# Identity transposes up to both seams of `expert_choice`, its bias as one fp32r product, its output statistics on ScalarE, late weight groups between its tiles

## The reference, cut to what matters

```python
def _L0_ffn_ref(x, router_w, router_b, expert_w, expert_b):
    logits = xf @ router_w + router_b
    S = jax.nn.softmax(logits, axis=-1)
    G, idx = jax.lax.top_k(S.T, k)              # 16 experts, k = 64 of 1024 tokens
    tokens = xf[idx]
    out = jnp.einsum('ekh,hd->ekd', tokens, expert_w) + expert_b
    weighted = G[..., None] * out
    y = jnp.zeros((bs, h), dtype=x.dtype).at[idx.reshape(-1)].add(weighted.reshape(-1, h))
...
x = x + _layernorm(_L0_ffn_ref(_layernorm(x, axis=-1), ...), axis=-1)
```

## Time and profile before

| | |
|---|---|
| median of 3 runs | 509.27 us (508.12 to 510.45) |
| the profiled execution | 510.88 us |
| its span, first to last instruction | 509.1 us |
| mean granted TensorE clock | 0.834 |
| busy: PE, PE weight loads, VectorE, ScalarE, GpSimd | 388.3, 301.1, 301.4, 242.1, 112.3 us |
| time mixing | up to 81.8 us of the span |
| `expert_choice` | 82.3 to 139.1 us |
| `delta_attention` | from 139.6 us |

### The profile page before, as it was taken

The page is one execution under the profiler, slowest core; times in us unless marked ns, Lnnn a source line. Parts: engine busy times, 40 slices in busy tenths (PEclk is TensorE's granted clock), DMA queues, the critical chain, the costliest instruction groups (busy, mean ns, idle before and its releaser), DMA issues. The chain is left out here.

```text
span 509.1 us, 9989 instructions
## 1 busy us (share of the span) xinstructions
PE 388.3 (76%) x4106; PEld 301.1 (59%) x4106; DVE 301.4 (59%) x649; ACT 242.1 (48%) x427; POOL 112.3 (22%) x132
## 2 busy tenths in 40 slices
PE   2999775999379977543218799952999999999990
PEld 1544565756267766522117545642888888888880
DVE  5899997371832665699994467686394311311126
ACT  2889754103334677566314356655855422222330
POOL 5490001000000001500005500000034565334540
PEclk9999988555868999955558957995899999999996
DMA  7890000000000000000000000000004400000002
GB/s 224 254 303 1 0 1 0 1 1 0 0 0 3 1 3 3 1 1 1 0 0 3 3 5 4 3 2 0 1 2 166 165 1 2 1 1 0 2 1 82
DMA packets 12489, 15.82 MB, mean 31 GB/s; under 512 B 2046, under 2 KB 10644, under 8 KB 12444
## 3 DMA queue, kind: packets, MB, share of 16 engines
q1 hardware_dynamic: 12444, 15.18, 9.3%
HBM read 14.09 MB, written 1.08 MB: 30 GB/s over the span
## 5 line engine op out<-in xcount | busy, mean ns | idle before, releaser
L2191 POOL TENSOR_TENSOR hidden_r<-third,hidden_r 128x512 fp32r<-128x512 f32 x31 | 41.2, 1331 | 141.7 <-ACT hidden_r L2143 141.7
L2256 DVE TENSOR_TENSOR third<-third,ps 128x512 f32<-128x512 f32 x32 | 22.0, 686 | 84.8 <-PE ps L2074 79.5
L2090 PEld LDWEIGHTS ps<-down_r,hidden_r 128*128 128x128 f32 x384 | 49.1, 188 | 3.2 <-POOL hidden_r L2191 0.9
L2090 PE MATMUL ps<-down_r,hidden_r 128*128 128x256 f32 x384 | 50.2, 280 | 0.7 <-POOL hidden_r L2191 0.7
L2074 PE MATMUL ps<-xm_r,gate_r 128*128 128x512 f32 x192 | 50.1, 397 | 0.0
L2074 PE MATMUL ps<-xm_r,up_r 128*128 128x512 f32 x192 | 49.9, 396 | 0.0
L2143 ACT CAST hidden_r<-third 128x512 fp32r<-128x512 f32 x32 | 19.9, 623 | 59.2 <-PE ps L2090 59.2
L2074 PEld LDWEIGHTS ps<-xm_r,up_r 128*128 128x128 f32 x192 | 36.9, 192 | 7.9
L1475 PE MATMUL ps<-ident,area 128*128 128x128 f32 x32 | 8.4, 413 | 40.4 <-DVE area L1801 40.4
L2074 PEld LDWEIGHTS ps<-xm_r,gate_r 128*128 128x128 f32 x192 | 34.5, 191 | 5.8 <-issue 0.2
L1475 PEld LDWEIGHTS ps<-ident,area 128*128 128x128 f32 x32 | 5.5, 207 | 43.2 <-DVE area L1801 43.2
(11 more groups left out here) (324 smaller groups left out, 845.6 us busy)
## 6 DMA issues: line engine op xcount, KB each, us to landing
stored<-share_dram SPq DMA_DIRECT2D x8, 512.0 KB, 5.4
stored<-in_L_ffn_sw_dram SPq DMA_DIRECT2D x3, 1024.0 KB
stored<-in_L_ffn_w_dram SPq DMA_DIRECT2D x1, 2048.0 KB
x<-L_attn_hidden_state_dram SPq DMA_DIRECT2D x4, 256.0 KB, 3.7
out_dram<-x SPq DMA_DIRECT2D x4, 256.0 KB, 2.5
w_nat<-in_L_attn_Wk_dram SPq DMA_DIRECT2D x1, 256.0 KB, 2.9
w_nat<-in_L_attn_Wv_dram SPq DMA_DIRECT2D x1, 256.0 KB, 3.1
w_nat<-in_L_attn_Wr_dram SPq DMA_DIRECT2D x1, 256.0 KB, 3.3
```

The source lines that it names most:

```text
L2090: last = nc.tensor.matmul(ps[:, t // 2, t % 2 * D:(t % 2 + 1) * D], hidden_r[:, n % 2, hp, t * P:(t + 1) * P], down_r[:, wp, a, :], start= ...
L2191: nc.gpsimd.tensor_tensor(hidden_r[:, n % 2, LO, :], hidden[:, n % 4, :], hidden_r[:, n % 2, HI, :], ALU.subtract).then_inc(hidden_lo, 1)
L2256: V.tensor_tensor(hidden[:, n % 4, :], gated[:, n % 2, :], ps[:, 4 + 2 * (n % 2) + 1, :], ALU.mult) \
```

## The change

- **First seam.** Time mixing ends with 40 transposes of the identity and not 24; `expert_choice` begins on TensorE with 14.
- **Second seam.** The transposes at the end of `expert_choice` are 30 and not 36, and wait for the first normalized tile of the output (`tail_normed`); `delta_attention` begins with 8.
- **Bias.** GpSimd splits the fp32 bias into three parts that fp32r holds exactly, in rows 0, 32 and 64 of `bias_r`, and makes `bias_rows`, which has ones in these rows and zeros elsewhere. The bias of a tile is then one fp32r product. `experts(0)` waits for the ten GpSimd instructions. `to_quarters` and `minus_before` are now made behind these, in `expert_choice`.
- **Late groups.** One group stands ahead of each of tiles 2 to 6, none behind tile 7.
- **Statistics.** ScalarE passes over each pair of finished tiles with `Identity` and sums (`accum_out`) the means, between its copies of the late groups; when all eight are there it makes the negative means (`z_centre`), and then passes over the tiles with `Square` and sums the variances. VectorE no longer takes them.
- The semaphores of the logarithm and the reciprocal of time mixing become one.

```diff
-        STAY_WARM = 24
+        STAY_WARM = 40
...
-    STAY_WARM = 36
+    STAY_WARM = 14, 30
...
+        z_moments = sem("z_moments")
+        bias_made = core.pool_count[0] + 10
+        masks_made = bias_made + 1 + QUARTERS
...
+                for n in range(STAY_WARM[0]):
+                    nc.tensor.transpose(ps[:, 7, 0:P], core.ident[:], core.ident[:])
...
-                    nc.tensor.matmul(z[:, t], core.ones[0:1, :], core.b_ec[0:1, 0:D], start=False, stop=True) \
+                    nc.tensor.matmul(z[:, t], bias_rows[:], bias_r[:], start=False, stop=True) \
                         .then_inc(z_done, 1)
 
+                pe.wait_ge(sem("masks_order"), bias_made)
                 experts(0)
...
-                for t in range(1, NT):
+                experts(1)
+                for n, t in enumerate(range(2, NT)):
+                    core.turn_groups(pe, core.turned_late[n:n + 1], LATE_BANKS)
                     experts(t)
-                core.turn_groups(pe, core.turned_late, LATE_BANKS)
-
+
+                pe.wait_ge(sem("masks_order"), masks_made)
                 pe.wait_ge(ties_counted, 1)
...
-                for n in range(STAY_WARM):
+                pe.wait_ge(sem("tail_normed"), TB + 1)
+                for n in range(STAY_WARM[1]):
                     nc.tensor.transpose(ps[:, PROB_BANK, 0:P], core.ident[:], core.ident[:])
...
+                link(nc.gpsimd.tensor_copy(bias_r[:], bias))
+                subtract(rest[:], bias, bias_r[:])
+                link(nc.gpsimd.tensor_copy(bias_r[own[1]], rest[own[1]]))
+                link(nc.gpsimd.tensor_copy(bias_r[own[2]], rest[own[2]]))
+                subtract(bias_r[own[2]], rest[own[2]], bias_r[own[2]])
+                link(nc.gpsimd.memset(rest[:], 0.0))
+                for q in range(3):
+                    link(nc.gpsimd.memset(rest[PAD * q:PAD * q + 1, 0:P], 1.0))
+                link(nc.gpsimd.tensor_copy(bias_rows[:], rest[:, 0:P]))
...
-                core.keep_groups(act, core.turned_late, LATE_BANKS)
+                for n, t in enumerate(range(0, NT, 2)):
+                    act.wait_ge(z_done, t + 2)
+                    for tile in (t, t + 1):
+                        nc.scalar.activation(xf[:, tile], z[:, tile], ACT.Identity, scale=1.0 / D,
+                                             accum_out=norm.mv[:, tile, 0:1]).then_inc(z_moments, 1)
+                    core.keep_groups(act, core.turned_late[2 * n:2 * n + 2], LATE_BANKS)
+                act.wait_ge(z_moments, NT)
+                nc.scalar.activation(centre[:], norm.mv[:, :, 0], ACT.Copy, scale=-1.0 / D ** 0.5) \
+                    .then_inc(z_moments, 1)
+                act.wait_ge(z_moments, NT + 1)
+                for t in range(NT):
+                    nc.scalar.activation(xf[:, t], z[:, t], ACT.Square, scale=1.0 / D ** 0.5, bias=centre[:, t:t + 1],
+                                         accum_out=norm.mv[:, t, 1:2]).then_inc(z_moments, 1)
                 norm.on_act(act, core.ln_eps[:])
...
-                dve.wait_ge(z_done, NT)
-                for t in range(NT):
-                    last = norm.tile_stats(z, t)
-                link(last)
-                link(norm.gather_stats())
+                dve.wait_ge(z_moments, 2 * NT + 1)
                 dve.wait_ge(limit_and_g, 2)
...
+    STAY_WARM = 8
...
+                    for n in range(STAY_WARM):
+                        nc.tensor.transpose(ps[:, 0, 0:P], ident[:], ident[:])
```

More of the change, by code:

```diff
@@ L172, in masks @@
         g = self.nc.gpsimd
-        count = [0]
-        def link(ins):
-            count[0] += 1
-            ins.then_inc(order, 1)
-            pool.wait_ge(order, count[0])
+        link = chain(pool, order, self.pool_count)
         def where(dst, op, fill, base, pattern, step):
@@ L800, in expert_choice @@
         limit = sb("limit", [P, 1])
+        centre = sb("z_centre", [P, NT])
+        to_quarters = sb("to_quarters", [PAD, P])
+        rest = sb("bias_rest", [P, D])
+        bias_r = own.enter_context(nc.sbuf_tensor("bias_r", [P, D], F32R))
+        bias_rows = own.enter_context(nc.sbuf_tensor("bias_rows", [P, P], F32R))
+        minus_before = sb("minus_before", [P, P])
         own_least = sb("own_least", [P, QUARTERS])
@@ L2303, in sandwich @@
         core.norm_after = Norm(core, "ln_after")
-        core.dve_count = [0]
+        core.dve_count, core.pool_count = [0], [0]
         core.weights(ins)
```

30 lines of the change are left out of this document (16 added, 14 removed).

## The result

The changed kernel takes **487.36 us** (median of 4 runs, 484.04 to 490.06), the kernel before beside it on the same chip 508.69 (4 runs, 506.31 to 510.45): a ratio of 0.958 with a 95% interval of 0.950 to 0.966. The profiled execution of after took 489.34 us (span 487.6), that of before 510.88 (509.1): 21.5 us less, where 16.9 were forecast. In the medians of this document a run that lies over 1.5% above the fastest of its kernel is counted (one of `n_groups`, 495.62, and one of `n_stats`, 493.72), in the ratios it is not.

What follows compares the result with a forecast made beforehand. TensorE at half clock was taken to bound expert_choice; 15.9 us there plus 1.0 at the second seam made 16.9, giving 494.0 from the profile or 492.4 from the median, so 493.0 us, range 487.5 to 501.5.

Steps and rivals of the forecast that it cites:

- Second seam: From expert_choice into attention: first projections nearer full clock, between 0 and 3.2 us gained, 1.0 taken.
- the sum for `expert_choice`: Root of the variances at the stage's end done at 114.8 instead of 130.72, 15.9 us sooner.
- it is not the bound: VectorE's selection in expert_choice: scan ends at 107.3, `tied` near 109, so VectorE does not set the end.
- Half-clock stretch: Behind the router's logits TensorE runs 3.3 us at half clock, losing 1.6 us.
- Tiles: Expert tiles on TensorE: 1.1 us each at full clock, 2.2 at half; the last ends at 106.2.
- Sums on ScalarE: Statistics passes over the expert tiles: 0.67 us each, bounds 0.47 and 1.07; 8.6 us from last tile to root.
- (d): Rival: ScalarE's sums each end in a drain and read, making the kernel slower, 513.3 us at pitch 1.4; chance 0.04.
- (b): Rival: no half-clock stretch behind the logits and a warm second seam, 488.6 us; chance 0.11.
- Table load: ScalarE's load before the root: 1.28 us, no drain added, no cover assumed.
- (a): Rival: clock falls at the first seam anyway and rises after some 7 us of tiles, 499.5 us; chance 0.20.
- (c): Rival: half clock throughout expert_choice's tiles and groups, gain 3.3 us, 506.0 us; chance 0.09.
- (e): Rival: TensorE stops for ScalarE's copies or GpSimd, losing 16 us, within 0.5% of 509.3; chance 0.04.

Runs made afterwards that it cites:

- n_groups: Changed kernel with the five late groups behind the last tile again, copied by ScalarE between sums and squares: 489.92 us.
- n_stats: Changed kernel with the outputs' statistics back on VectorE, groups still between the tiles: profiled expert_choice stage 38.83 us.
- n_seam1: Changed kernel without the first seam's added transposes (24 at time mixing's end, none at the head of expert_choice): 493.1 us.
- v_attn: Changed kernel with 16 and 24 identity transposes filling TensorE's two pauses in the attention stage: 482.33 us.
- b_bias: Kernel before with only the bias as one fp32r product: 14.0 us off the stage, 15 off the kernel.
- n_bias: Changed kernel with the old one-row fp32 bias product, operands for the new one still made: 500.97 us.
- x_select: Changed kernel with two of eight selection rounds on VectorE left out, so the output differs: `limit` 1.95 us and the root 0.66 us sooner.
- after_again: The changed kernel run once more, unaltered, to see the spread: 487.79 us.
- n_seam2: Changed kernel with the old second seam: 36 transposes that wait for nothing, none at the attention stage's head: 489.24 us.
- v_tail: Changed kernel with 28 more transposes between the last tile and the products for `limit`, and 58 instead of 30 at the stage's end: 487.70 us.
- b_seam1: Kernel before with only the first seam's transposes (40 and 14): logits 4.47 us sooner, stage 5.23 us shorter.

## Where the prediction was right, and where it failed

The sign and the two large mechanisms stood: the seam's clock, and the bias that keeps the clock down. The size did not: 493.0 us were forecast and 487.36 measured, 0.14 us below the range. The step that failed is the sum for `expert_choice`: 15.9 us were to be gained there and 20.4 were. It had three faults. TensorE's last tile was put 3.0 us too late, the sums on ScalarE behind it were priced 2.1 us too high, and "it is not the bound", of VectorE, did not hold in this execution.

**First seam: right.** Logits 4.4 us sooner was forecast, and 4.47 measured. The 16 transposes took 2.05 us (1.9), the 32 products 3.71 (3.7), the half-clock stretch behind them 3.3. `n_seam1` gives all of it back.

**Half-clock stretch: priced too high.** "3.3 us at half lose 1.6" took the stretch to lie on the tiles. It lay on 90.0 to 93.3, where TensorE ran tile 0 ahead of need and then waited for the probabilities; from tile 1, at 92.86, on it cost some 0.4. That it was as short as forecast is in part luck: in four other executions it is 6.8 us and the last tile some 2 us later, which moves the root by 1.2 us (28.97 in `v_attn`, 27.75 in after). With the long one the stage gains 19.0 to 19.2 us and not 20.4, still over 3 more than forecast.

**Tiles: right in kind, a little high.** 1.1 us a tile and 1.57 with a group were forecast, 0.98 and 1.42 measured: 0.9 us over the seven tiles and five groups. The 0.24 us taken for an fp32 pass was an upper bound; the passes of a tile in after start 0.21 apart. From the logits to tile 1 it took 2.78 us (90.08 to 92.86), and not the 3.6 that were carried over. Of these 0.8 us TensorE itself was 0.6: in the kernel before the probabilities were ready at 97.68 and it came to them at 98.31, behind tile 0's old bias product; in after it was 92.32 and 92.38. With the stretch, the last tile ended 20.9 us into the stage and not 23.9: 3.0 us.

**Bias: right in kind, and the largest part.** `b_bias` alone brings 14.0 us of the stage; `n_bias` shows that it is the clock far more than the product. The forecast said as much, but gave no share.

**Sums on ScalarE: mis-sized.** I took 0.67 with 0.47 as the lower bound. Measured: sums 0.37 apart, squares 0.45 to 0.46 (the eight of them and the reads end at 107.23). The read of the accumulator that rival (d) feared is there, 0.19 to 0.24 us, but it overlaps the next activation. The bound came from an activation with two per-partition operands; those with one or none are faster here. Squares ended 4.9 us behind the last tile and not 7.0.

**"It is not the bound": wrong where the last tile is early.** VectorE's scan came nearly as worked out: it ended 24.4 us into the stage, and was forecast 25.0. But with the last tile 3.0 us and the squares 2.1 us earlier than I had them, ScalarE's chain ended ahead of VectorE's: the selection and the pick products behind `limit` end last, by some 0.6 us, and that only because the clock fell among these products at 107.0. They took 0.93 + 0.99 us, where `x_select` has 0.61 + 0.61. In the executions with the long stretch ScalarE's chain ends last, as forecast. From the end of the last tile to the root done it took 7.1 us, where 8.6 were forecast: 1.5 less, and not 2.1.

Together 3.0 + 1.5 = 4.5 us: 20.4 measured in the stage, 15.9 forecast. In the profiled executions 0.9 more came from the earlier start of the stage, which is spread, and 0.7 less from the second seam. The other 1.0 us of the 5.6 is in the medians: that of after lies 1.98 us below its profiled execution, where 493.0 allowed 1.0. On which side of the range's end the median fell is chance, too: after_again gives 487.79, just inside. But the range had been drawn too high. Its lower end had no case with both the cheap sums and the cheap stretch; rival (b) with the bare pass of 0.47 is 486.6.

**GpSimd: right.** The bias operands were ready at 88.15, and no row of TensorE waits for them. **Second seam: open.** The head of the attention stage gained 3.3 us, just beyond my upper bound of 3.2; over the stage 0.3 was left, against 1.0 taken; by runs 1.45 us lie between `n_seam2` and after_again, whose runs overlap. **Table load: right.** No drain shows: in `x_select` ScalarE's last read ends at 107.67, the load starts at 107.69 and the root at 108.98, 1.29 us later. The Trainium skill ("ScalarE: Activation LUTs", "What ACT_TABLE_LOAD costs") has about 1.38 us of drain with each such load; this trace has no room for it. In after the load ends at 108.53, ahead of the root at 109.15, so that it cost nothing there.

**Rivals.** (b), 488.6, is nearest to the measured time, though not by its reason: the half-clock stretch was there. (a) is what `n_seam1` shows when forced, at 493.1 and not 499.5: there too the tiles ended 3.4 us sooner and the rest took 2.1 us less than (a) had. (c) did not come; `n_bias`, at 500.97 and not 506.0, is nearest to it, with the clock at 0.50 for 20.3 us. (d) falls with pitches of 0.37 and 0.46. (e) falls with TensorE's 8.70 busy us of 8.70.

## What to carry to other kernels

When TensorE is slow over a whole stage, look for the cheap odd instruction in its steady loop as well as for the pause ahead of it: a pass that keeps the clock down costs far more than its own row says. An edit that shortens one of two chains to the same join can bring nothing until both are short, so price them as a pair, and redo the question of who ends last with the lower bounds as well as the chosen values. Filling a pause of TensorE paid where long work followed it (`v_attn`), and cost where a late start had already taken up the pause (`v_tail`). And where the clock falls at other places in the next execution, compare two profiles only when their stretches at half clock are alike.

## What the runs showed of the hardware that was not expected

- One-row fp32 products between full ones kept TensorE at 0.50 for 20.3 us in which it waited for no other engine (`n_bias`), where the same tiles without them run at 1.00 from 93.4 on (after). The bias products of the eight tiles are all that differs. Their weights, and those of what follows them, are not loaded beside the running pass, so that each stands between short pauses; which property of them holds the clock is open.
- An activation with a sum of 128x256 from PSUM costs 0.37 us (Identity, constant scale) or 0.45 (Square with a bias column). Its read of the accumulator is a row of its own, 0.19 to 0.24 us, mostly beside the next activation.
- VectorE's four normalized tiles took 2.06 us at 82.81 in after, beside GpSimd's work on the bias, and 1.37 at 83.70 in the kernel before. GpSimd's work is the reason: `b_bias`, which adds the bias alone to the kernel before, has 2.07, and `b_seam1`, without it, 1.37. The rows' transposes still came in time: 2.76 us into the stage in both before and `b_bias`.
- The same code draws a half-clock stretch of 3.3 or 6.8 us at the same place, three times the one and four times the other, and so a last tile that moves by 2 us with no edit ahead of it.
